# Mamba loop: GpSimd multiplies states with C four units at a time, with other ring sizes and later folds

## What is computed

```python
xi, z = split(x @ in_w.T)                      # 256 channels each
xc = silu(conv4(xi) + cb)
dt, Bm, Cm = split(xc @ xp_w.T)                # 8, 16, 16
delta = softplus(dt @ dtw.T + dtb)
for t in range(512):                           # h: 256 channels x 16 states
    h = exp(delta[t] * A) * h + (delta[t] * xc[t]) * Bm[t]
    y[t] = sum over states of h * Cm[t] + xc[t] * D
x = (y * silu(z)) @ ow.T
```

## Time and profile before

| | before |
|---|---|
| device time, median of 3 | 1371.69 us (1370.31 to 1371.77) |
| span of the profiled execution | 1350.2 us |
| TensorE busy | 1167.2 us, 86% |
| VectorE busy | 1108.2 us, 82% |
| ScalarE busy | 1039.4 us, 77% |
| GpSimd busy | 951.5 us, 70% |
| Mamba steps, first to last scan | 599.2 to 1335.0 us |

### The profile page before, as it was taken

One profiled execution on the slowest core, in us unless ns is written; L12 is line 12 of the kernel. 1 busy time (PEld: TensorE's weight loads), 2 busy tenths in 40 slices (PEclk: granted clock), 3 DMA queues, 4 the chain that ended last, 5 costly groups with the idle time before them and its releaser, 6 DMA issues. The chain is left out here.

```text
span 1350.2 us, 21804 instructions
## 1 busy us (share of the span) xinstructions
PE 1167.2 (86%) x6683; PEld 616.3 (46%) x6683; DVE 1108.2 (82%) x1571; ACT 1039.4 (77%) x1817; POOL 951.5 (70%) x856
## 2 busy tenths in 40 slices
PE   6367899999729999988999999999999999999875
PEld 3362244444415567634444444444444454444432
DVE  6866899999676323258999999999999999999996
ACT  3346999999452223279999999999999999999991
POOL 7561511121473633239999999999999999999995
PEclk9696999999858999998999999999999999999998
DMA  2032233433118204244144414442443244324410
GB/s 69 1 115 79 90 108 112 122 112 97 30 34 296 71 24 133 74 113 94 45 103 104 105 45 92 102 107 56 92 107 87 59 109 102 75 57 107 102 55 16
DMA packets 86062, 118.22 MB, mean 88 GB/s; under 512 B 16053, under 2 KB 47232, under 8 KB 85576
## 3 DMA queue, kind: packets, MB, share of 16 engines
q1 hardware_dynamic: 79688, 99.59, 28.2%
q0 software_dynamic: 6272, 17.38, 4.4%
HBM read 90.80 MB, written 26.92 MB: 87 GB/s over the span
## 5 line engine op out<-in xcount | busy, mean ns | idle before, releaser
L1880 POOL TENSOR_TENSOR hcm<-hs,Cc 128x1024 f32<-128x1024 f32 x256 | 601.3, 2367 | 23.9 <-DVE hs L2312 14.0
L2312 DVE TENSOR_TENSOR_SCAN hs<-decay,dbx 128x512 f32<-128x512 f32 x512 | 588.4, 1200 | 29.4 <-PE dbx L2003 14.0
L2194 ACT ACTIVATE decay<-dtr,a_cur 128x512 f32<-128x512 f32 x512 | 356.2, 717 | 4.5 <-DVE hs L2312 4.2
L2003 PEld LDWEIGHTS dbx<-ident_sb,scaled 128*128 128x128 f32 x2048 | 229.0, 142 | 284.2 <-DVE hs L2312 142.3
L2003 PE MATMUL dbx<-ident_sb,scaled 128*128 128x128 f32 x2048 | 305.5, 282 | 36.7 <-DVE hs L2312 33.9
L2172 ACT ACTIVATE scaled<-duT,BT 128x256 f32<-128x256 f32 x514 | 234.4, 502 | 0.1
L2019 PE MATMUL y_bank<-hcm,fold_sb 128*32 128x512 f32 x1024 | 138.9, 615 | 7.2 <-POOL hcm L1880 7.2
L920 ACT ACTIVATE ex<-tt 128x1024 f32<-128x1024 f32 x128 | 138.3, 1080 | 5.6 <-DVE tt L970 4.8
L1934 PE MATMUL slots<-XT,w_tap 128*128 128x512 f32 (+1 forms) x240 | 122.5, 597 | 20.1 <-DVE scaled L2303 18.9
L1869 POOL TENSOR_SCALAR scaled<-duT,BT 128x256 f32<-128x256 f32 x270 | 127.0, 483 | 13.9 <-ACT duT L2134 13.9
L969 DVE TENSOR_TENSOR tt<-bank_l,gt 128x512 f32<-128x512 f32 x128 | 87.3, 682 | 21.5 <-PE bank_l L813 18.8
(11 more groups left out here) (342 smaller groups left out, 1886.9 us busy)
## 6 DMA issues: line engine op xcount, KB each, us to landing
dtr<-dt_turn SPq DMA_DIRECT2D x60, 512.0 KB, 8.8
Cc<-bc_turn SPq DMA_DIRECT2D x256, 64.0 KB, 2.0
dt_turn<-dt SPq DMA_DIRECT2D x15, 512.0 KB, 2.8
conv_row<-in_conv_row SPq DMA_DIRECT2D x4, 512.0 KB, 6.1
shares_of_tokens<-zeros SPq DMA_DIRECT2D x2, 1024.0 KB, 9.9
w_rg<-in_w_rg SPq DMA_DIRECT2D x8, 256.0 KB, 2.7
w_ru<-in_w_ru SPq DMA_DIRECT2D x8, 256.0 KB, 3.0
w_rd<-in_w_rd SPq DMA_DIRECT2D x8, 256.0 KB, 2.9
```

The source lines that it names most:

```text
L1880: nc.gpsimd.tensor_tensor(hcm[:, r - 1:r + 1, :], hs[:, p % HR - 1:p % HR + 1, :], Cc[:, k:k + 1, :].broadcast_to([P, 2, 512]), ALU.mult). ...
L2003: last = nc.tensor.transpose(dbx[bank_of[p]][:, P * kk:P * kk + P], scaled[:, buffer_of(l, b, k), kk, g, :, :].rearrange("p j c -> p (j c) ...
L2194: nc.scalar.activation(dec[:, p % DR, :], dtr[:, b % 2, g, :], ACT.Exp, scale=a_cur[:, 4 * g + k:4 * g + k + 1]).then_inc(s_dec, 1)
L2312: nc.vector.tensor_tensor_scan(hs[:, p % HR, :], dec[:, p % DR, :], dbx[bank_of[p]][:, :], 0.0, ALU.mult, ALU.add).then_inc(s_sc, 1)
```

## The change

- State buffers HR: 8 to 12. Product buffers MR: 12 to 8. A state's buffer is now counted over all steps (`state_of`), since 32 isn't a multiple of 12.
- GpSimd multiplies four units by one instruction of 128x2048 instead of two by one of 128x1024: eight in a step instead of sixteen. Each waits for the four scans and for the fold of the quad two before.
- GpSimd's small multiplies (`scale_by_b`) are grouped after these: three after units 3 and 7 (group 2 of the same batch), four after 23 and 27 and two after 31 (the next batch). In the first step all sixteen of group 1 stand ahead of the loop.
- The folds stand later in TensorE's order: (0, 1) at v = 16 instead of 14, (1, 0) at 20 instead of 18, (1, 1) at 24 instead of 22, (2, 0) at 28 instead of 25, (2, 1) at 0 of the next step instead of 30, (3, 0) at 3 instead of 1, (3, 1) at 7 instead of 6. Fold (0, 0) stays at 12. `out_proj` stands at 12 and 13 instead of 11 and 12, `start_y` at 10 and 11 instead of 9 and 10.
- `gate_y` stands after scans 8 and 9 instead of 7 and 8, `copy_out` after decay 18 instead of 16.

```diff
--- before.py
+++ after.py
@@ -1677,7 +1677,7 @@
         st5 = ExitStack()
         with st5:
             UN = 32
-            DR, HR, MR, GROUPS = 8, 8, 12, 4
+            DR, HR, MR, GROUPS = 8, 12, 8, 4
             y_bank = [st5.enter_context(nc.psum_tensor(f"y_bank{i}", [P, 512], fp32)) for i in range(2)]
             dbx = [st5.enter_context(nc.psum_tensor(f"dbx{i}", [P, 512], fp32)) for i in range(3)]
             slots = st5.enter_context(nc.psum_tensor("slots", [P, 3, 512], fp32))
@@ -1733,6 +1733,7 @@
             units = [(p // 8, p % 8) for p in range(UN)]
             buffer_of = lambda l, n, k: (4 * (4 * l + n) + k) % 3
             ring_of = lambda l, b, p: (UN * (4 * l + b) + p) % MR
+            state_of = lambda l, b, p: (UN * (4 * l + b) + p) % HR
 
             at = lambda l, n, per, k: l * (4 * per) + (per * n + k)
             by_parity = lambda l, n, per: l * (2 * per) + per * (n // 2 + 1)
@@ -1746,7 +1747,7 @@
             first = lambda l, b: isinstance(l, int) and l == 0 and b == 0
             layer = lambda l, n: l + 1 if n >= 4 else l
             more = lambda l, n: not (l == 3 and n >= 4)
-            hc_after = [p // 2 * 2 + 2 for p in range(UN)]
+            hc_after = [p // 4 * 4 + 4 for p in range(UN)]
 
             with nc.Block() as block:
                 @block.sync
@@ -1872,31 +1873,28 @@
                     def weigh(l, b, p):
                         k, g = units[p]
                         pool.wait_ge(s_sc, at(l, b, UN, p + 1))
-                        if g % 4 == 1:
-                            wait(pool, s_fm, at(l, b, 8, p // 4 - 2))
-                        if g == 1:
+                        wait(pool, s_fm, at(l, b, 8, p // 4 - 1))
+                        if g == 3:
                             pool.wait_ge(s_cb[k], at(l, b, 64, 64))
-                        r = ring_of(l, b, p)
-                        nc.gpsimd.tensor_tensor(hcm[:, r - 1:r + 1, :], hs[:, p % HR - 1:p % HR + 1, :],
-                                                Cc[:, k:k + 1, :].broadcast_to([P, 2, 512]), ALU.mult).then_inc(s_hc, 2)
-
-                    own_scales = {1: (2, (2, 3)), 3: (2, (4, 5)), 5: (2, (6, 7))}
+                        r, i = ring_of(l, b, p), state_of(l, b, p)
+                        nc.gpsimd.tensor_tensor(hcm[:, r - 3:r + 1, :], hs[:, i - 3:i + 1, :],
+                                                Cc[:, k:k + 1, :].broadcast_to([P, 4, 512]), ALU.mult).then_inc(s_hc, 4)
+
+                    own_scales = {3: (2, (2, 3, 4)), 7: (2, (5, 6, 7))}
+                    next_scales = {23: (1, (0, 1, 2, 3)), 27: (1, (4, 5, 6, 7)), 31: (2, (0, 1))}
 
                     def step(l, b):
-                        for p in range(1, UN, 2):
+                        for p in range(3, UN, 4):
                             weigh(l, b, p)
-                            if first(l, b) and p in (1, 3):
-                                for x in range(4 * p - 4, 4 * p + 4):
-                                    scale_by_b(l, b, 1, x)
-                            elif first(l, b) and p in (5, 7):
-                                for x in range(2 * p - 10, 2 * p - 6):
+                            if first(l, b) and p == 3:
+                                for x in range(8):
                                     scale_by_b(l, b, 2, x)
                             elif p in own_scales and not first(l, b):
                                 k, some = own_scales[p]
                                 for x in some:
                                     scale_by_b(l, b, k, x)
-                            if p >= 23 and more(l, b + 1):
-                                k, some = (1, (p - 23, p - 22)) if p < 31 else (2, (0, 1))
+                            if p in next_scales and more(l, b + 1):
+                                k, some = next_scales[p]
                                 for x in some:
                                     scale_by_b(l, b + 1, k, x)
 
@@ -1904,6 +1902,8 @@
                     pool.wait_ge(s_dut, 1)
                     for x in range(10, 16):
                         scale_by_b(0, 0, 0, x)
+                    for x in range(16):
+                        scale_by_b(0, 0, 1, x)
                     for b in range(4):
                         step(0, b)
                     for l in range(1, 4):
@@ -2047,26 +2047,26 @@
                                 if v in (24, 25, 26, 27):
                                     xi(l, n + 1, 0, ((24, 25, 26, 27).index(v),))
                             if not first(l, b):
-                                if v == 1:
+                                if v == 0:
+                                    fold_quad(l, b - 1, 2, 1)
+                                if v == 3:
                                     fold_quad(l, b - 1, 3, 0)
-                                if v == 6:
+                                if v == 7:
                                     fold_quad(l, b - 1, 3, 1)
-                                if v in (11, 12):
-                                    out_proj(l, b - 1, v - 11)
-                            if v in (9, 10):
-                                start_y(l, b, v - 9)
+                                if v in (12, 13):
+                                    out_proj(l, b - 1, v - 12)
+                            if v in (10, 11):
+                                start_y(l, b, v - 10)
                             if v == 12:
                                 fold_quad(l, b, 0, 0)
-                            if v == 14:
+                            if v == 16:
                                 fold_quad(l, b, 0, 1)
-                            if v == 18:
+                            if v == 20:
                                 fold_quad(l, b, 1, 0)
-                            if v == 22:
+                            if v == 24:
                                 fold_quad(l, b, 1, 1)
-                            if v == 25:
+                            if v == 28:
                                 fold_quad(l, b, 2, 0)
-                            if v == 30:
-                                fold_quad(l, b, 2, 1)
                             if l == 3 and b == 3 and v in (3, 6, 24):
                                 turn_out((3, 6, 24).index(v))
 
@@ -2102,6 +2102,7 @@
                     for l in range(1, 4):
                         for b in range(4):
                             step(l, b)
+                    fold_quad(3, 3, 2, 1)
                     fold_quad(3, 3, 3, 0)
                     fold_quad(3, 3, 3, 1)
                     for h in range(2):
@@ -2229,7 +2230,7 @@
                                     copy_dut(l, n)
                                 if w >= 28:
                                     scale_by_b(l, n, 1, w - 20)
-                            if w == 16 and not first(l, b):
+                            if w == 18 and not first(l, b):
                                 copy_out(l, b - 1)
                             if w in (2, 4) and not first(l, b):
                                 for x in (w + 10, w + 11):
@@ -2309,7 +2310,7 @@
                         dve.wait_ge(s_dec, at(l, b, UN, p + 1))
                         dve.wait_ge(s_bx, at(l, b, UN, p + 1))
                         wait(dve, s_hc, at(l, b, UN, hc_after[p - HR] if p >= HR else hc_after[p - HR + UN] - UN))
-                        nc.vector.tensor_tensor_scan(hs[:, p % HR, :], dec[:, p % DR, :], dbx[bank_of[p]][:, :], 0.0, ALU.mult, ALU.add).then_inc(s_sc, 1)
+                        nc.vector.tensor_tensor_scan(hs[:, state_of(l, b, p), :], dec[:, p % DR, :], dbx[bank_of[p]][:, :], 0.0, ALU.mult, ALU.add).then_inc(s_sc, 1)
 
                     def step(l, b):
                         n = b + 1
@@ -2317,8 +2318,8 @@
                             scan(l, b, u)
                             if u in (20, 22, 24, 26) and more(l, n):
                                 scale_by_b(l, n, (u - 20) // 2)
-                            if u in (7, 8) and not first(l, b):
-                                gate_y(l, b - 1, u - 7)
+                            if u in (8, 9) and not first(l, b):
+                                gate_y(l, b - 1, u - 8)
                             if l == 3 and b == 3 and u in (9, 14, 29):
                                 gate_out((9, 14, 29).index(u))
                             if u in (9, 10) and more(l, n):
```

## The result

The changed kernel takes 1382.64 us (median of 4 runs, 1378.80 to 1385.56), the kernel before, run beside it, 1371.00 (4 runs, 1369.36 to 1371.77). The ratio is 1.0086, 95% interval 1.0063 to 1.0109: slower by 11.6 us. 1378.7 with a range of 1362 to 1389 was forecast, and "slower" with 0.60.

The account below looks back on a forecast made before the run. Four nearly full engines in the Mamba loop, with VectorE halted by TensorE's order in a gap-free stretch; 14 steps x 0.5 = 7.0 us, ends 0, added to 1371.7 gives 1378.7 us, range 1362 to 1389.

Parts of the forecast that it names:

- The mechanism and its place: TensorE's gap-free stretch from tap to unit 8: later folds delay inputs by 0.99 us each, so VectorE halts longer.
- The step: One Mamba-loop batch step between line 2303 multiplies: 45.30 us becomes 45.8, +0.5, from 0.3 to 0.8.
- The duT copy: ScalarE's copy that VectorE's multiply at 906.53 wants: shifted later, up to 0.2 us more per step, taken as 0.05.
- x_proj: TensorE's 1.84 us operation in the stretch: z comes 1 us later, yet x_proj still finds silu of z at 877.1.
- GpSimd's multiply: Four-unit multiply in the loop: 4.56 us from the 512-to-1024 slope; hidden under other engines, so 0 by itself.
- rival (c): GpSimd slower when wide, or ring waits loop with TensorE: at 5.0 us a multiply, 28 us more, 1400; chance 0.05.
- The last step: Kernel's end: last multiply 2.2 us longer, earlier GpSimd work ending sooner; taken as 0, from -3 to +5.
- rival (d): Shared SBUF port alone: last-step VectorE multiplies with two SBUF inputs wait on longer GpSimd instructions; +5, 1377; chance 0.05.
- The base of the sum: Whole kernel: profiled span 1350.2 us plus 21.5 lying around it in the median 1371.69, untouched by the change.
- The stretch starts at the tap: TensorE's gap-free work begins at the tap waiting for VectorE's multiply after scan 22; otherwise the forecast breaks.
- Rival (b): Fold (1,1) at the tap falls into TensorE slack: step 0.16 us shorter, 1369.5; chance 0.2 with its like.
- Rival (a): GpSimd sets the loop's pace: 1.1 us won in each of 14 steps, 1356, down to 1348; chance 0.15.

Follow-up runs that it names:

- experiment 1: Kernel before with only the changed kernel's order of folds, out_proj, start_y, gate_y and copy_out; GpSimd multiply and rings as before: 1383.54 us, ratio 1.0106.
- experiment 2: Changed kernel (four-unit multiply, 12 state and 8 product buffers) with the old order of folds, out_proj, start_y, gates and copy_out: 1371.19 us, ratio 1.0009.
- experiment 5: Kernel before with fold (2,0) moved from v = 25 to v = 24, ahead of the tap: 1367.40 us, ratio 0.9992.
- experiments 3: Changed kernel with only fold (1,1) moved back from v = 24 to v = 22, ahead of the waiting tap: 1373.79 us, ratio 1.0016.
- 9: Kernel before with fold (2,0) at v = 24 ahead of the tap and (2,1) at 28 instead of 30, ahead of z: 1359.26 us, ratio 0.9948.
- experiment 10: Kernel before, two-unit multiplies, with (2,0) ahead of the tap, (2,1) ahead of z and (3,1) behind unit 8: 1356.12 us, ratio 0.9922.
- experiments 6: Wide multiply and its rings, old order, but (2,0) ahead of the tap, (3,1) behind unit 8, gates, start_y and out_proj one later: 1370.62 us, ratio 1.0016.
- 8: Kernel before with fold (3,1) moved from unit 6 to behind unit 8; gates, y groups and output projection one later: 1367.85 us, ratio 1.0008.
- 11: Wide multiply and its rings, with (2,0) ahead of the tap, (2,1) behind unit 28, (3,1) behind unit 8: 1367.70 us, ratio 1.0007.
- 4: Changed kernel with folds (1,1) at 22, (2,0) at 25, (2,1) at 1, (3,0) at 7, (3,1) at 8: 1377.32 us, ratio 1.0058.

## Why the prediction was right, point by point, and where it was not

**The mechanism and its place** were right, and are shown and not only argued: the order alone, with GpSimd untouched, gives the changed kernel's halts and its loss (experiment 1), and the other half of the change gives no loss in the steps (experiment 2). The halt before scan 2 went, scans 30, 1 and 8 got theirs, with 0.48, 0.85 and 0.20 us where 0.4, 1.1 and 0.2 to 0.3 had been worked out, and TensorE has no gap from the tap to unit 8.

**The step** was forecast at 45.8 (+0.5, 0.3 to 0.8) and is 45.93 (+0.63). The halts of the changed step are 0.48 + 0.85 + 0.18 + 0.20 + 0.12 = 1.83, those of before 1.31, so +0.52. The last 0.1 is the overlap between neighbouring instructions that is lost at each halt (a scan alone is 1.22 us, in a row 1.11). There are five halts for three; the 0.18 holds its own lost overlap, which leaves one more. I counted the overlap for the kernel before and not for the halts that the change adds. The duT copy was taken at 0.05 and is 0.12.

**x_proj** came 11.11 us behind the tap, before 11.16: as forecast. It now stands right behind ScalarE's silu of z (756.28 + 1.02 against 757.43), whose slack the later z has used up.

**GpSimd's multiply** was taken at 4.56 from the slope between 512 and 1024 elements, and is 4.561. So rival (c), a slower wide form, falls away. The wait of 1.9 us at units 20 to 23 is 1.99. The Trainium skill (GPSIMD Engine Reference, "Elementwise — side-by-side cycle accounting") has 4497 ns for this size; the trace has 64 ns more, and as forecast the time doesn't hang on it.

**The last step** was taken at 0 and costs 2.63. This is the term that failed. The prediction saw the last multiply 2.2 us longer (4.50 against 2.34) but set against it that GpSimd's earlier work ends sooner. That can't help: in both kernels the last multiply waits for the last scan, 2.92 and 2.93 us. The multiply makes 2.15 of the 2.63. Another 0.45 is no part of the change's work: the last four transposes (L2080) took 1.11 us at a granted clock of 0.50 (1.2 GHz) and 0.66 in before at 1.00 (2.4 GHz), each after a wait of 0.69 for ScalarE, and they took 1.11 in experiment 1 too, whose multiply is the old one. VectorE's rows of the end, changed kernel:

```profile
1325.29 3.45 DVE L2337 TENSOR_TENSOR dtr<-dtr,GATE 128x512 f32<-128x512 f32 x1
...
1334.93 1.30 DVE L2337 TENSOR_TENSOR dtr<-dtr,GATE 128x512 f32<-128x512 f32 x1
...
1354.04 2.90 DVE L2337 TENSOR_TENSOR dtr<-dtr,GATE 128x512 f32<-128x512 f32 x1
...
1365.86 1.29 DVE L2290 TENSOR_TENSOR zs<-y_bank,zs 128x512 f32<-128x512 f32 x2 [6.68 <-PE y_bank L2019]
```

The last gates wait 6.68 us for the fold behind that multiply, before 4.54. The three multiplies with both inputs in SBUF, the shared port of rival (d), sum to 7.65 us; before they were 0.85, 4.01 and 2.91, 7.77. So the port costs nothing more here. Nor does it over all thirteen kernels: the three sum to 7.07 to 9.84 us in the six with two units a multiply and to 7.41 to 8.60 in the seven with four, with means of 8.1 and 8.0. The Trainium skill (SBUF — State Buffer, "Who interferes with whom") has a VectorE instruction with two SBUF inputs contend with a GpSimd instruction that reads SBUF. The trace agrees in that such a multiply takes 0.69 us alone and up to 5.48 beside GpSimd (experiment 5); that longer GpSimd instructions make it wait longer, as rival (d) had it, no run here shows.

**The base of the sum** was read wrongly. The 21.5 us between the profiled span of before and its median are not work around the span: in the runs whose span is listed, time less span is 1.8 us (1378.80 and 1377.0). The profiled execution of before was itself a quick one, with its first scan at 599.2 us where all other profiled kernels have 611 to 619, in work that the change doesn't touch; with its 1350.2 us of span it was quicker than every timed run of that kernel (1363.54 at the least). The sum was unharmed, since the difference was added to the median.

**"The stretch starts at the tap"** was the statement that the forecast was said to hang on, and it is only part of the truth. There are three starts: the tap, z, which needs VectorE's fourth scaled multiply, and unit 0, which needs scan 29. For this change all readings give nearly the same, since a whole fold more came ahead of z and z came 1.14 us later (9.32 us behind the second scaled multiply, before 8.18), too late for either wait to matter. For undoing it they differ, which is why experiments 3 and 5 missed: in 5 the wait ahead of z took the whole gain, and in 3 and 9 the wait of unit 0 left 0.5 of 0.99. Rival (b) of the prediction had named scan 29 as that limit, at 0.64. Rival (b) named a gain of 0.16 us a step if fold (1,1) fell into slack; put there on purpose, the step is 45.44, 0.14 above before, because scan 29 holds unit 0 and the later (3,0), (3,1) and gates stay.

**Rival (a)**, GpSimd sets the pace, is refuted for the two kernels: in 2 its work fell by 1 us a step and the step stayed. But it was the next bound, about 0.7 us below (44.64 in experiment 10), and it is not quite where I put it, at 44.8: its idle time in before is 0.7 us a step (7.57 us in a window of 500), more than the 0.45 that I called all of it, since short ones beside its small operations are not printed as waits.

What stays open: why TensorE's clock falls in some steps of experiments 6, 8 and 11 and not in others, with the same program and the same wait before it; what the rings cost apart from the width; and how much of the loss in experiment 1 is the folds' and how much that of the operations moved with them. In 4 the long steps go with a late copy of dt, and the clock falls in five of the six.

## What to carry to other kernels

When four engines are within 4% of each other, read one step as a timetable and look for the points where the in-order engine itself waits: work ahead of such a point is free up to its slack, work behind it is paid up to the next such point, and there may be several (here three, which left 0.54 of a fold's 0.99 us). Take an engine's pace from its own rows, not from those of an engine that it holds back only now and then. Before an engine's instruction is made wider because that is less work, ask whether that engine is late anywhere; a wider one delivers its first result later, holds its buffers longer and lengthens the end of the kernel. Here moving two folds of 0.99 us across one wait was worth 0.5%, and with a third move 0.8% in all, where 20 us less work on an engine was worth nothing.
